# Key differences loaded behind the row sums, and the output of a half head copied from PSUM by VectorE

## The reference

```python
q = (x @ W_q + b_q) @ W_s; k = x @ W_k + b_k; v = x @ W_v + b_v   # B 2, T 2048, 16 heads of 16
scores = jnp.einsum('bhqd,bhkd->bhqk', q, k) / jnp.sqrt(jnp.float32(Hd))
attn = jax.nn.softmax(scores, axis=-1)
out = jnp.einsum('bhqk,bhkd->bhqd', attn, v)
...
return out @ W_o + b_o
```

## Time and profile before

| | |
|---|---|
| median of 3 runs | 1703.52 us (1702.05 to 1704.21) |
| profiled execution | 1699.82 us, its span 1697.9 us |
| busy, share of the span | TensorE 97%, VectorE 86%, ScalarE 80%, GpSimd 15% |
| mean granted clock of TensorE | 0.978 of full speed |

### The profile page before, as it was taken

How to read it: one execution, slowest core, us unless ns; L and a number is a source line. 1 busy time by engine, 2 the same in 40 slices (tenths; PEclk the granted TensorE clock), 3 DMA queues, 4 the chain that set the end, 5 groups by cost and what they waited for, 6 DMA issues and landing times. The chain is left out here.

```text
span 1697.9 us, 45489 instructions
## 1 busy us (share of the span) xinstructions
PE 1641.8 (97%) x17243; PEld 939.6 (55%) x17243; DVE 1464.5 (86%) x2913; ACT 1359.1 (80%) x2640; POOL 254.9 (15%) x323
## 2 busy tenths in 40 slices
PE   7999999999999999999999999999999997699998
PEld 5645555555455555554555555455555586488887
DVE  5679999999999999998999999899999386777773
ACT  2328999999899999998999999899999824365563
POOL 0443222100010000001000000100000012144533
PEclk9999999999999999999999999999999997699999
DMA  7771644222332332223222333242220331235432
GB/s 267 217 239 50 156 79 103 47 49 48 58 58 46 56 61 49 47 49 68 51 45 45 52 58 57 54 62 50 50 45 12 113 118 63 99 99 138 108 71 35
DMA packets 101287, 134.53 MB, mean 79 GB/s; under 512 B 27164, under 2 KB 73820, under 8 KB 97964
## 3 DMA queue, kind: packets, MB, share of 16 engines
q1 hardware_dynamic: 90444, 115.33, 29.7%
q0 software_dynamic: 7808, 14.68, 3.9%
q10 hardware_dynamic: 2816, 1.61, 0.3%
HBM read 89.64 MB, written 40.63 MB: 77 GB/s over the span
## 5 line engine op out<-in xcount | busy, mean ns | idle before, releaser
L1215 ACT ACTIVATE pt<-ps 128x512 f32<-128x512 f32 x2048 | 1073.9, 603 | 79.4 <-PE ps L699 60.3
L1238 DVE TENSOR_REDUCE pmax<-ps 128x1 f32<-128x512 f32 x1626 | 1008.2, 683 | 57.7 <-PE ps L1300 56.4
L699 PE MATMUL ps<-qp,kp 50*128 50x512 f32 x2048 | 710.4, 447 | 1.1 <-DMA qp<-m_rows 0.6
L1300 PE MATMUL ps<-kp,qp 48*128 48x512 f32 x1812 | 638.4, 449 | 5.8 <-DVE pmax L1238 5.7
L1318 PE MATMUL ps<-pt,v_st 128*32 128x256 f32 (+1 forms) x10752 | 592.2, 336 | 0.7 <-ACT pt L1215 0.7
L1300 PEld LDWEIGHTS ps<-kp,qp 48*128 48x128 f32 x1812 | 295.7, 185 | 229.1 <-DVE pmax L1238 137.1
L699 PEld LDWEIGHTS ps<-qp,kp 50*128 50x128 f32 x2048 | 332.5, 185 | 137.2 <-ACT pt L1215 122.5
L1318 PEld LDWEIGHTS ps<-pt,v_st 128*32 128x32 f32 x10752 | 266.2, 109 | 246.6 <-issue 178.0
L291 POOL CAST m_parts<-rowmax_t 128x32 fp32r<-128x32 f32 x64 | 13.5, 211 | 788.4 <-DVE rowmax_t L323 788.3
L1242 DVE CUSTOM_DVE_ANT_0 stage_b<-ps,stage_b 128x512 f32<-128x512 f32 x186 | 126.4, 680 | 0.5 <-issue 0.5
L1201 ACT ACTIVATE stage_b<-ps 128x512 f32<-128x512 f32 x186 | 113.9, 612 | 0.0
(11 more groups left out here) (243 smaller groups left out, 1497.7 us busy)
## 6 DMA issues: line engine op xcount, KB each, us to landing
kp<-k_parts SPq DMA_DIRECT2D x186, 128.0 KB, 4.5
v_all<-L_ffn_w SPq DMA_DIRECT2D x16, 1024.0 KB, 6.3
qp<-q_parts SPq DMA_DIRECT2D x186, 64.0 KB, 4.0
k_parts<-pt SPq DMA_DIRECT2D x16, 512.0 KB, 3.7
q_parts<-pt SPq DMA_DIRECT2D x16, 512.0 KB, 3.1
o_rows<-o_sb SPq DMA_DIRECT2D x64, 128.0 KB, 4.1
sums_c<-o_rows SPq DMA_DIRECT2D x512, 0.5 KB
kd<-kd_parts SPq DMA_DIRECT2D x186, 32.0 KB, 1.8
```

The costliest lines, as they stand in the source:

```text
L699: nc.tensor.matmul(bank(n % SCORE_BANKS), kp[rows, h % NBUF, kt * P:(kt + 1) * P], qp[rows, h % NBUF, f * CH:(f + 1) * CH], start=True, st ...
L1215: nc.scalar.activation(pt[:, s % PTS, half * CH:(half + 1) * CH], bank(n % SCORE_BANKS), ACT.Exp, scale=SCALE).then_inc(scores_out, 1)
L1238: v.reduce_max(pmax[:, u % 2, at:at + 1], part_slot(n), AX.X).then_inc(groups_out, 1)
L1300: mm(part_slot(n), qp[rows, r, col:col + P], keys, start=True, stop=True).then_inc(groups_full, 1)
```

## The change

It does two things. The six DMA transfers of the key differences, for the head after next, go to a later place in the same turn of SP's loop: behind the output and row sums of the last unit, and behind the inverses where there are any. And the copy of `acc` to `o_sb` is made by VectorE, in its queue behind the reduction of part 19 (`COPY_PART` = 2 * 8 + 3) of the parts stream, for all units but the last; ScalarE's copy ahead of the exponential of chunk 3 goes, and keeps only that of the last unit. Shape and semaphores of the copy stay.

```diff
+COPY_PART = 2 * LEAD + 3
...
                         place_maxima(sp, u + 1)
-                    if u % HALVES == 0 and u // HALVES + 2 < G:
-                        load_differences(sp, u // HALVES + 2)
                     if u > 0:
                         load_output(u - 1)
...
                         finish_group(u - 2)
+                    if u % HALVES == 0 and u // HALVES + 2 < G:
+                        load_differences(sp, u // HALVES + 2)
...
                 for n in range(STEPS * 2):
-                    if n % UNIT_CHUNKS == BLOCK and n > UNIT_CHUNKS:
-                        take_output(n // UNIT_CHUNKS - 1)
...
+                def copy_output(u):
+                    dve.wait_ge(pv_done, (u + 1) * BLOCKS)
+                    if u > 1:
+                        dve.wait_ge(o_stored[u % 2], (u // 2) * 16)
+                    v.tensor_copy(o_sb[:, u % 2, :], acc).then_inc(acc_out, 1)
...
                         reduce_part(n)
+                    if p == COPY_PART and u > 1:
+                        copy_output(u - 2)
...
                 join(UNITS - 1)
+                copy_output(UNITS - 2)
```

## The result

The changed kernel takes 1754.87 us (median of 4 runs, 1753.91 to 1757.76) against 1703.87 of the kernel before: 51 us more, ratio 1.0304 with an interval of 1.0286 to 1.0321. The forecast was 1759, range 1734 to 1776. The profiled execution takes 1754.82 us, 55 more than that of before; its span is 1753.0.

The account below looks back on a forecast made before the run. TensorE was taken to set the pace, VectorE and ScalarE waiting for it. Profiled 1699.82 + 68 (copy stalls) - 12 (key differences) = 1755.8; with 3.7 for the median, 1759 us, range 1734 to 1776.

Parts of the forecast that it names:

- The stall: At each half head's end TensorE's value products wait for VectorE's copy: 1.12 us worked out, 62 x 1.10 = +68 us.
- where in VectorE's queue it stands: Copy behind the reductions of parts 16 to 19 in VectorE's queue: ends at 613.08, products at 613.33 instead of 612.21.
- the 0.80 of the earlier trace: Least stall found, at the boundary near 498 us where VectorE had waited ahead of part 19: 0.80 us.
- No making up: After each boundary VectorE and ScalarE run dry, so TensorE's full 1.12 us is lost in each half head.
- The absorbed rival: Weight-load waits are slack that a late TensorE gets back: fully, median 1691 (3%); half, median 1725 (7%).
- The key differences: Moved behind the row sums on SP's queue, they end VectorE's three waits for the sums: -12 us.
- The reciprocal's cost at the copy: VectorE's reciprocal, 0.55 us, pushes back the copy that follows it: 3 x 0.5 = 1.5 us.
- ScalarE's copy at nothing: Removing 63 copies of 0.33 us from ScalarE's queue gains nothing, since ScalarE waits for TensorE later anyway.
- the 20 of the rival: Rival that ScalarE paces the half heads: losing its copies saves 0.33 x 62 = 20.5 us, median 1670; 3%.
- VectorE's work at nothing: VectorE's added copy per half head, 0.42 us, counted only through the end that TensorE waits for.
- The sum: Whole run: 1699.82 + 68 - 12 = 1755.8 for the profiled execution; 3.7 more for the median, 1759.
- The clock: Rival: 1.1 us stalls lower TensorE's clock in a fifth of half heads, 28 us more, median 1787; 5%.

Follow-up runs that it names:

- the last run: Kernel before, ScalarE keeping the copy, with an added VectorE reduction of 256 columns behind part 19 that nobody reads: 1710.24 us, ratio 1.0044.

## Why the prediction was right

*The stall.* Forecast 1.12 us at the boundary that was worked out, 1.10 on average, 62 times: +68. Measured: the period grew by 1.12 where it was read, the stalls by the waits are 1.09 each, the copy alone costs 70, and on top of the key differences 67. In the traces of the last two, 61 half heads take 1222.43 us in the change and 1155.64 with the key differences alone, 1.10 more each. Each step held: the copy takes 0.41 (0.42 assumed from a copy of another type), the products follow its end by 0.26 (0.25), and it stands behind the reduction of part 19. Moving it one reduction earlier took 38 us away (37), which is the step "where in VectorE's queue it stands" shown by itself. The spread was smaller than the prediction thought: the products follow the last matmul by 1.48 at most boundaries and by 1.23 at the least, so stalls as short as the 0.80 of the earlier trace rows hardly occur.

*No making up.* VectorE and ScalarE run dry and wait for TensorE, as forecast, and nothing that can be seen is given back: at full clock the half head is longer by the whole stall, and by the whole extra reduction in the copy behind part 20. The absorbed rival falls.

*The key differences.* Forecast -12; measured alone -15 in the medians, and 1699.82 - 1687.16 = 12.7 between the profiled executions, from which the forecast was worked out. The sums land ahead of VectorE's turn, by little (0.3 us of wait are left in the change), and the three long half heads go with their lower clock. The reciprocal's cost at the copy, 1.5 us in the forecast, belongs only to the change. It came to 1.5, but by luck: six inversions fall into the loop, not three, and at their boundaries the products follow the last matmul by some 1.73 instead of 1.48, 0.25 more and not 0.5.

*ScalarE's copy at nothing.* With the stall gone and ScalarE relieved, the kernel is no faster than with ScalarE's copy. That run also gave VectorE its extra work, which cost 7 us by itself in the last run; 7 less the 6 measured leaves about 1 us for ScalarE's relief, an estimate from two differences of some us, against the 20 of the rival. (The prediction calls ScalarE the busiest engine of the half head; by the earlier trace rows that is TensorE, and ScalarE is second.)

*VectorE's work at nothing.* That step was not quite right. I priced VectorE's added work only by its end; where no stall hides it, it costs 6 to 7 us. In the change itself TensorE's stall covers it. Which waits make up these 6 to 7 us was not taken apart.

*The sum.* For the profiled execution 1755.8 were forecast and 1754.82 came. That they agree within 1 us is in part luck, since executions of the changed kernel alone lie up to 4 us apart. The median forecast is 4 us too high, since I added the 3.7 us by which the profiled execution of before lay under its median; that of after lies at its own. The runs suggest that this spread belongs to the waits for the sums: the kernel before ranges from 1698.41 to 1712.65 in 17 executions, the one with the key differences moved from 1686.80 to 1691.61 in six. That is not shown by itself.

*The clock.* I gave 5% to many stalls that lower it. At stalls of 1.1 us it fell in one half head; at 1.7 us, behind part 20, often enough for half of that kernel's extra time. So the rival's mechanism is there, 0.6 us of stall away, and the prediction had no row that told how near it was.

The fastest version of all that were run is the kernel before with the key differences moved and nothing else, 1687.92 us, faster than both.

## What to carry to other kernels

Where three engines are all 95% busy, shares don't tell what a moved instruction costs: look for who waits for its end, and put its new start behind everything that is ahead of it in the new queue. Work that another engine waits for has a window in a queue, here one of the five places tried: too early it waits for its input and holds up what follows, too late it holds up the reader. And take a change of two parts apart: one half of this one was worth 15 us and was hidden under the other.

## What the runs showed of the hardware

The granted clock fell far more often with half as much again of stall. With stands of TensorE of about 1.1 us in each of 62 half heads it fell to 1.2 GHz in one of them (mean clock 1.00 in that stretch); with 1.7 us in each, for part of 20 of them (mean 0.97), which were 1.4 to 3.1 us longer than the others. Before the change it had fallen behind two of the three stands of some 3 us.

A value product started 0.25 to 0.26 us behind the end of the copy it waited for, with either engine's copy, but a part matmul started 0.05 behind the end of the reduction it waited for (647.79 to 647.84 above, and 0.05 to 0.06 at the same place of all 62 half heads with the copy behind part 16). Why the two differ was not tested. And with the copy behind part 18 a stall with two conditions was put down by the profile to ScalarE in 46 of 48 waits, where VectorE's copy explains it.
